# A mixture-of-experts router in fp32r: tokens as the stationary operand, 42 router columns moving

## The reference

```python
def _L0_ffn_ref(x, gate_w, expert_fc1, expert_fc2, expert_proj, shared_fc1, shared_fc2, shared_proj, shared_gate_w):
    xf = x.reshape(-1, c)
    router = xf @ gate_w.T                                # 8 columns
    probs = jax.nn.softmax(router.astype(jnp.float32), axis=1)
    top_p, top_i = jax.lax.top_k(probs, TOPK)             # TOPK = 2
    combine = zeros((n, E)).at[arange(n)[:, None], top_i].set(top_p)
    h = silu(einsum('nc,efc->enf', xf, expert_fc1)) * einsum('nc,efc->enf', xf, expert_fc2)
    y = einsum('ne,enc->nc', combine, einsum('enf,ecf->enc', h, expert_proj))
    shared = silu(xf @ shared_fc1.T) * (xf @ shared_fc2.T) @ shared_proj.T
    return y + sigmoid(xf @ shared_gate_w.T) * shared     # 1 column
x = x + tanh(g_xattn[0]) * attention(_layernorm(x), ctx)
x = x + tanh(g_ffn[0]) * _L0_ffn_ref(_layernorm(x), ...)
```

## Time and profile before

| | us |
|---|---|
| median of 3 runs | 286.82 (286.31 to 286.86) |
| the profiled execution | 286.08 |
| its span, first to last instruction | 284.3 |
| PE busy | 271.9 (96%) |
| DVE busy | 209.7 (74%) |
| ACT busy | 164.2 (58%) |
| POOL busy | 134.6 (47%) |

### The profile page before, as it was taken

One profiled execution on the slowest core, in us unless ns is written; L12 is line 12 of the kernel. 1 busy time (PEld: TensorE's weight loads), 2 busy tenths in 40 slices (PEclk: granted clock), 3 DMA queues, 4 the chain that ended last, 5 costly groups with the idle time before them and its releaser, 6 DMA issues.

```text
span 284.3 us, 5839 instructions
## 1 busy us (share of the span) xinstructions
PE 271.9 (96%) x1788; PEld 246.7 (87%) x1788; DVE 209.7 (74%) x683; ACT 164.2 (58%) x369; POOL 134.6 (47%) x160
## 2 busy tenths in 40 slices
PE   3999999999999999999999999999999999999994
PEld 3799889889897777898788888899999999998883
DVE  6959767888778779578767858777777878763365
ACT  2875687777455395652245555567676666654330
POOL 2241913714575555663430000087787878776140
PEclk9999999999999999999999999999999999999998
DMA  7452263130046226424335653578887888766796
GB/s 198 186 190 86 75 221 94 59 131 0 23 110 250 78 76 211 154 68 127 127 91 203 221 182 101 161 122 135 139 135 139 134 138 135 119 71 71 265 399 227
DMA packets 25022, 40.18 MB, mean 141 GB/s; under 512 B 2976, under 2 KB 18976, under 8 KB 24992
## 3 DMA queue, kind: packets, MB, share of 16 engines
q1 hardware_dynamic: 16272, 27.43, 30.1%
q0 software_dynamic: 7152, 9.57, 19.9%
q10 hardware_dynamic: 1568, 2.80, 2.7%
HBM read 22.68 MB, written 17.11 MB: 140 GB/s over the span
## 4 chain that ended last, share of the span: by engine, by line
PE 81%; DVE 7%; DMA 5%; ACT 4%; issue 2%; ACTq 0%; DVEq 0%
PE bank L441 62%; PE bank L718 7%; DMA ew_hi<-y_d 3%; PE bank L449 3%; PE bank L817 3%; PE bank L771 3%; DVE work L1482 2%; ACT sh_hi L848 1%; DVE sh_lo L1119 1%; DMA consts_sb<-consts_dram 1%; PE bank L528 1%; ACT ew_hi L848 1%; DVE ew_lo L1119 1%; PE bank L598 1%; ACT work L1028 1%
## 5 line engine op out<-in xcount | busy, mean ns | idle before, releaser
L1685 POOL DMA_INDIRECT y_d<-work,dest_of_slot x39 | 60.5, 1552 | 55.4 <-DMA y_d<-work 38.9
L441 PE MATMUL bank<-ew_hi,xt_hi 128*128 (+2 forms) x172 | 53.9, 323 | 1.1 <-DVE xt_lo L1119 0.7
L441 PE MATMUL bank<-ew_lo,xt_hi 128*128 (+2 forms) x172 | 51.7, 301 | 0.0
L441 PE MATMUL bank<-ew_hi,xt_lo 128*128 (+1 forms) x133 | 40.6, 305 | 0.0
L1645 POOL DMA_INDIRECT xs_d<-xn_all,slot_of_pair x32 | 33.8, 1057 | 10.2 <-issue 7.3
L1119 DVE TENSOR_TENSOR xt_lo<-bank,xt_hi 128x256 fp32r<-128x256 f32 (+2 forms) x90 | 35.6, 397 | 3.6 <-ACT xt_hi L848 2.4
L441 PE MATMUL bank<-xt_hi,sw_hi 128*128 128x512 f32 x88 | 34.8, 395 | 0.2 <-issue 0.2
L848 ACT ACTIVATE xt_hi<-bank 128x256 fp32r<-128x256 f32 (+1 forms) x90 | 32.9, 410 | 2.9 <-PE bank L817 1.1
L441 PE MATMUL bank<-xt_lo,sw_hi 128*128 128x512 f32 x88 | 34.5, 392 | 0.0
L441 PE MATMUL bank<-xt_hi,sw_lo 128*128 128x512 f32 x88 | 34.3, 390 | 0.0
L441 PEld LDWEIGHTS bank<-ew_hi,xt_hi 128*128 128x128 f32 (+1 forms) x172 | 32.4, 189 | 1.8 <-DVE xt_lo L1119 0.9
(11 more groups left out here) (163 smaller groups left out, 667.3 us busy)
## 6 DMA issues: line engine op xcount, KB each, us to landing
work<-xs_d SPq DMA_DIRECT2D x39, 136.0 KB
weight_stage<-ew_dram SPq DMA_DIRECT2D x10, 486.5 KB, 3.6
y_d<-work SPq DMA_DIRECT2D x6, 512.0 KB
work<-ctx_t_dram SPq DMA_DIRECT2D x4, 512.0 KB, 3.2
ew_hi<-y_d ACTq DMA_DIRECT2D x4, 512.0 KB, 7.1
ew_hi<-y_d SPq DMA_DIRECT2D x4, 512.0 KB, 7.9
xn_all<-x_dram SPq DMA_DIRECT2D x3, 512.0 KB, 6.0
xs_d<-pad_row SPq DMA_DIRECT2D x9, 136.0 KB, 2.4
```

The source lines that it names most:

```text
L441: last = nc.tensor.matmul(dst, a, b, start=(n == 0), stop=(n == len(pairs) - 1))
L1685: nc.gpsimd.indirect_dma_start(out=y2_d, out_offset=bass.IndirectOffsetOnAxis(ap=IX[:, n:n + 1], axis=0), in_=EY[:, n % 4, :], in_offset=None,
```

## The change

`router(c)` and ACT's copy of the logits go, with their semaphores (`p_rt`, `a_lg`), and so do the four transposes. In their place `logits(c)` takes each block of 128 tokens as the stationary operand and moves 42 columns of `RW` (`RW_USED`; 41 are used, one more makes the number even): per block four products (two halves of the width, high and low of the tokens) that accumulate 128 x 42 in bank 7 where DVE read its logits before. That is 16 products with 16 loads per chunk. They stand where the transposes stood. `attend(c, 2)` no longer waits for ACT's copy. Logits wait directly for the router's low part, for the normalized tokens (`v_x2t`), for the reader of bank 7 (`v_x2`), and in the last chunk, as before, for `v_pos`.

```diff
+RW_USED = RW_ROWS + 1
-        LGT = WK[0:RW_ROWS, 4096:4608]
@@ PE
-                if j >= 2 and c > 0:
-                    waits = waits + [(0, a_lg, c) if j == 2 else (0, v_lg, c)]
+                if j == 3 and c > 0:
+                    waits = waits + [(0, v_lg, c)]
-            def router(c):
-                waits = [(0, v_x2t, 2 * c + 2), (0, rw_lo, 1), (0, v_x2, 4 * min(c + 1, LAST) + (1 if c < LAST else 4))]
-                last = chain(B[6][0:RW_COLS, :],
-                             [(RW[:, k, :], XT[b][:, c, k, :]) for k in range(KD) for b in range(2)], waits)
-                last.then_inc(p_rt, 1)
             def logits(c):
-                pe.wait_ge(a_lg, c + 1)
+                pe.wait_ge(rw_lo, 1)
+                pe.wait_ge(v_x2t, 2 * c + 2)
                 pe.wait_ge(v_x2, 4 * c + 6 if c < LAST else 4 * c + 4)
                 if c == LAST:
                     pe.wait_ge(v_pos, LAST)
                 for j in range(TPC):
-                    last = nc.tensor.transpose(B[7][:, j * 2 * RW_LO:j * 2 * RW_LO + RW_ROWS], LGT[:, j * P:(j + 1) * P],
-                                               ident[0:RW_ROWS, 0:RW_ROWS])
+                    last = chain(B[7][:, j * 2 * RW_LO:j * 2 * RW_LO + RW_USED],
+                                 [(XT[b][:, c, k, j * P:(j + 1) * P], RW[:, k, 0:RW_USED]) for k in range(KD) for b in range(2)])
                 last.then_inc(p_lg, 1)
@@ PE, the loop over c
                 if c > 1:
                     route(c - 2)
-                if c > 0:
-                    router(c - 1)
                 values(c, 2)
@@ PE, the last chunk
             fc(0, 3, (0,))
-            router(LAST)
             fc(0, 3, (1,))
             logits(LAST)
@@ ACT
-            def logits(c):
-                act.wait_ge(p_rt, c + 1)
-                act.wait_ge(p_lg, c)
-                copy(LGT, B[6][0:RW_ROWS, :]).then_inc(a_lg, 1)
-                if c > 0:
-                    logits(c - 1)
-                        logits(LAST)
```

More of the change, by code:

```diff
@@ L240, in build @@
         p_vo, a_wvo, v_wvo = map(sem, ("p_wvo", "a_wvo", "v_wvo"))
[L242 to L245, removed]
+        p_xt, p_qk, p_v, p_sc, p_pt, p_av, p_x2t, p_lg = map(
+            sem, ("p_xt", "p_qk", "p_v", "p_sc", "p_pt", "p_av", "p_x2t", "p_lg"))
+        a_xt, a_ct, a_qk, a_v, a_exp, a_pt, a_x2t = map(
+            sem, ("a_xt", "a_ct", "a_qk", "a_v", "a_exp", "a_pt", "a_x2t"))
         v_st1, v_mv1, v_xn, v_xt, v_qk, v_v, v_mx, v_pt = map(
```

## The result

| | before | after |
|---|---|---|
| median of 22 runs each, us | 286.97 | 288.05 |
| profiled execution, us | 286.08 | 286.79 |
| its span | 284.3 | 285.0 |

The ratio of after to before is 1.0042 with a 95% interval of 1.0024 to 1.0059: slower by 1.2 us (0.7 to 1.7). The forecast was 287.4, its range 286.6 to 288.8.

What follows compares the result with a forecast made beforehand. PE, busy for 96% of the span, was taken to bound the kernel. 0.08 + 0.08 - 0.62 + 1.07 = +0.61 us, added to the median of 286.82, gave 287.4, range 286.6 to 288.8.

Steps and rivals of the forecast that it cites:

- The pace of a short product: New logits products on PE: 0.112 us each, set by the 128-column load; 16 take 1.79 us a chunk.
- rival B: Each short product is dearer: at 0.15 us the time is 289.7, at 0.224 it is 294.5; chance 0.13.
- rival D: Loads run ahead and the stream sets the pace, 0.03 to 0.06 us; sum -0.38 to -0.86; chance 0.04.
- Chunks 0 and 1: Logits blocks of these chunks: PE's +0.33 us nearly hidden by ACT and PE's later wait, leaving +0.08 each.
- rival A: No cover in chunks 0 and 1, as PE is the bound: +0.33 twice, sum +1.11, 287.9 us; chance 0.20.
- the exponential: In chunks 0 and 1, ACT's projection copy was to start right behind the route's exponential, which holds ACT.
- Chunk 2: Values and ACT's copies come 0.93 us earlier, products run while attend waits; attend's fourth product 96.83 instead of 97.45: -0.62.
- Chunk 3: PE newly stands 0.6 us for VectorE's slots (bank 7), then runs the products, without cover: +1.07 us.
- rival C: Chunk 3's wait is not new or has slack behind it: chunk 3 +0.33, sum -0.13, 286.7 us; chance 0.13.
- the sum: All four chunks together: 0.08 + 0.08 - 0.62 + 1.07 = +0.61 us.
- the only risk: Granted clock, at 2.4 GHz in all slices: new stop of 0.6 us and shorter products might affect it; put at nothing.

Runs made afterwards that it cites:

- 64 columns: The changed kernel with 64 instead of 42 columns moved per short product, the other 22 of no use; one execution, 287.91 us.
- 32-product traces: Changed kernel with the last chunk's logits in bank 6 (no stop) and each of their products made twice; 289.00 us, ratio 1.0071 to before.
- the two wide products: Changed kernel plus two unread 512-column products into bank 6, ahead of the last chunk's wait for `v_pos`; 286.92 us, ratio 1.0017 to before.

## Why the prediction was right, and where it fell short

**Right, each by its own row.** The pace of a short product (0.112) and what sets it, the load: shown by the timeline, and by 64 columns at the same pace. This rules out rival B (a dearer product) and rival D (0.03 to 0.06). Chunks 0 and 1 at +0.08 each, the rest hidden behind ACT and the wait: +0.08 and +0.09, again +0.08 and +0.10 in the second trace of the changed kernel; rival A had +0.33. Of the way there one point was off: the exponential no longer holds ACT's copies, the end of the projection's products does. Chunk 2 at -0.62: -0.65 to -0.67 in all nine traces that have it. Chunk 3 at +1.07 with a new stop of 0.6: +1.09 or +1.10 in five traces, the stop 0.57 or 0.58, and 0.8 of it goes with the wait, which rules out rival C.

**Wrong: one step.** It is the last sentence ahead of the sum: the new stop of 0.6 us and the short products are "the only risk" for the granted clock, "and I put it at nothing". The risk was named and given no price and no rival of its own. Measured, it is a third of the executions (17 of 52 with the stop) times 1.6 us (1.0 to 1.8 by comparison), about 0.5 us on the mean: nearly as much as the whole sum. The argument for nothing was that the clock stood at its upper level in all slices of before, and that says only what before's mix of products does. That the range held the result is luck as far as this goes: it reached up to rival A, whose mechanism is not there, and rival A's 287.9 is even nearer to the 288.05 than the forecast is; the forecast of 287.4 is nearer to the executions at full clock (287.66 on the mean) than to all. Part of the remainder is the anchor: the 287.4 was added to a median of 286.82 from three runs, and that of 22 is 286.97.

What stays open: where in the changed kernel itself the clock falls, since no profile of it caught one of its seven or four executions (that it is behind chunk 3's block is argued from the 64-column and the 32-product traces, and from no version without the stop having it with 16 products); why one execution has it and the next not; what the two wide products do to it, for which 12 executions are few; and how much of the sum reaches the end, since traces at full clock give +0.46 and +0.60 for the same kernel up to 114.9 us, and their times +0.33 and +0.64.

## What to carry to other kernels

Swapping operands to move few columns turns a product paced by its stream into one paced by its load: count loads (0.112 us for each 128 x 128 of fp32r here), not columns. The same block is worth -0.66 us where PE would have waited anyway and +1.1 us where it uncovers a wait that the removed work had hidden, so ask of each place separately and change only those that gain. And where an edit puts a stop next to a row of short products, look at the granted clock of every execution, not at one profile: a trace at full clock can show half of the loss.

## What the runs showed of the hardware that was not expected

- The granted clock fell to 1.2 GHz behind a stop with 16 short products (stops of 0.31 to 0.69 us in two kernels' traces, the fall up to 1.1 us behind the products), and at the end of 32 short products in which PE was never idle (115.54 to 118.95 and 52.23 to 55.65 among the former, 116.92 to 120.33 the latter). The engine had worked at 2.4 GHz up to there.
- It is a matter of the execution: 17 of 52 with the stop, 5 of 7 with 32 products, 0 of 48 with 16 products and no stop. With the stop it cost 1.0 to 1.8 us on the mean of a comparison, and of the five traces with chunk 3's block placed as in the change and the stop unfilled, four don't have it.
- The mean granted clock of these executions is 0.992 to 0.994, so close to 1 that it is easily passed over.
- Moving 64 columns instead of 42 costs nothing in pace as long as each product brings its own load of 128 columns.
